# Written first, on row groups: the bias and the push of the expert layer, in a six-stage transformer kernel

## The reference

```python
def _L1_ffn_ref(x, router_w, router_b, expert_w, expert_b):
    logits = jnp.einsum('bsd,ed->bse', x, router_w) + router_b
    probs = jax.nn.softmax(logits, axis=-1)
    weights = jnp.max(probs, axis=-1)
    top1 = jnp.argmax(probs, axis=-1)
    y_all = jnp.einsum('bsd,eod->bseo', x, expert_w) + expert_b
    y = jnp.take_along_axis(y_all, top1[:, :, None, None], axis=2)[:, :, 0, :]
    return y * weights[:, :, None]
...
    x = x + 0.5 * _L0_ffn_ref(_layernorm(x, axis=-1), ...)
    x = x + _L0_attn_ref(_layernorm(x, axis=-1), ...)
    x = x + 0.5 * _L0_ffn_ref(_layernorm(x, axis=-1), ...)
    x = x + 0.5 * _L1_ffn_ref(_layernorm(x, axis=-1), ...)
    x = x + _L1_attn_ref(_layernorm(x, axis=-1), ...)
    x = x + 0.5 * _L1_ffn_ref(_layernorm(x, axis=-1), ...)
```

## Time and profile before

| | us |
|---|---|
| median of 3 runs | 1593.41 (1593.11 to 1596.53) |
| profiled execution | 1591.5, of which the span is 1589.6 |
| first expert stage | about 1181 to 1250 of the span |
| second expert stage | about 1518 to the end of the span |
| TensorE busy (matmul) | 1541.5, 97% |
| VectorE busy | 1260.2, 79% |
| ScalarE busy | 936.1, 59% |
| GpSimd busy | 935.5, 59% |
| one batch of the first expert stage | 8.18 |

### The profile page before, as it was taken

One profiled execution on the slowest core, in us unless ns is written; L12 is line 12 of the kernel. 1 busy time (PEld: TensorE's weight loads), 2 busy tenths in 40 slices (PEclk: granted clock), 3 DMA queues, 4 the chain that ended last, 5 costly groups with the idle time before them and its releaser, 6 DMA issues. The chain is left out here.

```text
span 1589.6 us, 43810 instructions
## 1 busy us (share of the span) xinstructions
PE 1541.5 (97%) x15808; PEld 922.1 (58%) x15808; DVE 1260.2 (79%) x2662; ACT 936.1 (59%) x1826; POOL 935.5 (59%) x806
## 2 busy tenths in 40 slices
PE   7999999999999899799999999999999999999999
PEld 4666666666666666566666666666654434444444
DVE  7976776777877788786777777768778899999877
ACT  6755555555656344365555555556553388888842
POOL 2865756757754399775766756657456334444453
PEclk9999999999999999999999999999999899999999
DMA  4300000000001242100000000000001121112011
GB/s 163 106 8 5 7 0 7 7 0 7 8 1 34 53 84 67 42 6 3 8 1 7 7 0 7 7 0 8 5 12 31 44 61 37 39 39 62 9 42 60
DMA packets 74315, 43.34 MB, mean 27 GB/s; under 512 B 53818, under 2 KB 70842, under 8 KB 74052
## 3 DMA queue, kind: packets, MB, share of 16 engines
q1 hardware_dynamic: 74180, 41.56, 10.9%
HBM read 10.47 MB, written 2.10 MB: 8 GB/s over the span
## 5 line engine op out<-in xcount | busy, mean ns | idle before, releaser
L618 POOL TENSOR_TENSOR scratch<-scratch 128x512 f16<-128x512 f32 x379 | 441.6, 1166 | 375.4 <-ACT scratch L826 375.2
L1395 DVE SCALAR_TENSOR_TENSOR scratch<-psum,scratch 128x512 f32<-128x512 f32 x512 | 352.4, 689 | 235.8 <-PE psum L1979 213.4
L821 ACT ACTIVATE scratch<-psum 128x512 f32<-128x512 f32 x512 | 305.2, 597 | 394.9 <-PE psum L1979 394.0
L2021 PE MATMUL psum<-ffn_down_hi,scratch 128*128 128x128 f16 x2048 | 369.3, 219 | 0.3
L2023 PE MATMUL psum<-ffn_down_hi,scratch 128*128 128x128 f16 x2048 | 369.2, 219 | 0.0
L2022 PE MATMUL psum<-ffn_down_lo,scratch 128*128 128x128 f16 x2048 | 369.2, 219 | 0.0
L826 ACT ACTIVATE scratch<-scratch 128x512 f16<-128x512 f32 x512 | 318.6, 622 | 12.0 <-DVE scratch L1395 11.7
L2021 PEld LDWEIGHTS psum<-ffn_down_hi,scratch 128*128 128x128 f16 x2048 | 200.3, 98 | 59.1 <-POOL scratch L618 0.7
L2022 PEld LDWEIGHTS psum<-ffn_down_lo,scratch 128*128 128x128 f16 x2048 | 200.4, 98 | 58.0
L2023 PEld LDWEIGHTS psum<-ffn_down_hi,scratch 128*128 128x128 f16 x2048 | 200.4, 98 | 0.0
L1977 PE MATMUL psum<-x_hi,ffn_gate_hi 128*128 (+1 forms) x512 | 194.5, 380 | 1.5 <-ACT scratch L821 1.5
(11 more groups left out here) (223 smaller groups left out, 2703.8 us busy)
## 6 DMA issues: line engine op xcount, KB each, us to landing
scratch<-scratch SPq DMA_DIRECT2D x96, 128.0 KB, 2.7
raw<-in_ffn_w_dram SPq DMA_DIRECT2D x8, 768.0 KB, 4.2
ffn_up_hi<-scratch SPq DMA_DIRECT2D x32, 128.0 KB, 2.8
x_tok<-in_x_dram SPq DMA_DIRECT2D x8, 256.0 KB, 7.2
out_dram<-x_tok SPq DMA_DIRECT2D x7, 256.0 KB, 2.2
raw<-in_lin_dram SPq DMA_DIRECT2D x1, 1092.0 KB
x_hi<-scratch SPq DMA_TRANSPOSE x46, 2.3
x_lo<-scratch SPq DMA_TRANSPOSE x46, 2.3
```

Of the source, the lines that this page charges most:

```text
L618: pool.tensor_tensor(h_lo[r], h32[r], h_hi[r], ALU.subtract).then_inc(s_plo, 1)
L821: act.activation(gate_act[k % 2], bank(k % 2), ACT.Silu, scale=W_DOWN).then_inc(s_s, 1)
L1395: dve.scalar_tensor_tensor(h32[k % HSLOTS], bank(5 + k % 2), W_DOWN, gate_act[k % 2], ALU.mult, ALU.mult).then_inc(s_h, 1)
L2021: pe.matmul(dst, h_hi[r][:, cols], hi, start=k % FC == 0 and n == 0, stop=False, skip_group_check=True)
```

## The change

TensorE writes the bias and the push first. They stand in four groups of 32 rows (`E_GROUP`), each with the bias rows of one half (`e_bias`, placed by twelve small DMAs), and one push of four matmuls with 512 columns opens the banks of two tiles; the full products are then added to them (`start=not opened`). The mask `e_not` is written 16 times over, 32 columns apart in four groups of which the first 8 columns hold it, so that its transposition fills the rows of the four groups. Three pairs of banks take turns (`expert_banks`), and `picked_before` gives the pick for which a tile has to wait. The first and last tiles of the first stage, and the batch of the second stage that goes on beside the attention's end, keep another order. VectorE's `select` moves from behind pick 1 to behind pick 0, `prep_bn` from pick 0 to pick 1, `statistics` from pick 2 to pick 1. ScalarE's `x_upper` moves ahead of the first `weigh`, its `others` behind `weigh` 2, with 128 rows instead of 8. GpSimd's `x_lower` moves ahead of `add`. TensorE's loop is written out, and the router's bias is one matmul of 32 columns instead of four of 8.

```diff
-E_OUT = 2.0 ** 15
+E_OUT = 2.0 ** 14
+E_PUSH = 2.0 ** 16 - 2.0 ** 12
+E_GROUP = 32
...
-        e_not = carve(SUB * E, F16)
+        e_not = raw[:, 0:S // 2].bitcast(F16)
+        e_bias = raw[:, S // 2:S // 2 + BANK // 2].bitcast(F16)
...
+        def expert_banks(t):
+
+            if t < 2:
+                return t
+            if t < NS - 3:
+                return (2, 1, 0)[(t - 2) % 3]
+            if t < NS + SUB:
+                return t % 2
+            return (t - NS - SUB) % 3
+
+        def picked_before(t):
+
+            return 3 + max([s for s in range(t) if expert_banks(s) == expert_banks(t)], default=-1)
...
+            turn_x(3, 0)
+            sp.wait_ge(s_erows, 3)
+            sp.wait_ge(s_blo, 2)
+            for i in range(4):
+                c = slice(i % 2 * BANK, (i % 2 + 1) * BANK)
+                row = i * E_GROUP
+                sp.dma_start(e_bias[row:row + E, :], bias_w[0:E, c]).then_inc(s_ebias, 16)
+                sp.dma_start(e_bias[row + E:row + E + 1, :], bias_w[32:33, c]).then_inc(s_ebias, 16)
+                sp.dma_start(e_bias[row + E + 1:row + E + 2, :], bias_w[64:65, c]).then_inc(s_ebias, 16)
+            for b in range(1, NB):
...
                 for b in range(NB):
                     if b:
-                        add(b - 1)
                         if b + 2 < last:
                             x_lower(n0 + SUB * (b + 2))
+                        add(b - 1)
                     if b + 3 < last:
                         prep_rstd(n0 + SUB * (b + 3))
                         norm(b + 3)
...
-                def others(b, odd, at=4):
+                def others(b, odd, at=6):
                     act.wait_ge(s_eoutp, b + 1)
                     if not isinstance(b, int) or b > 1:
                         act.wait_ge(s_ey, SUB * b - SUB)
-                    act.activation(e_out[odd][0:E, :], bank(at)[0:E], ACT.Copy, scale=E_OUT).then_inc(s_eout, 1)
+                    act.activation(e_out[odd], bank(at), ACT.Copy, scale=E_OUT).then_inc(s_eout, 1)
...
-                        if k == 1 and prep and not (isinstance(b, int) and b == 0):
+                        late = use and isinstance(b, int) and b == 1
+                        if k == (1 if late else 0) and prep and not (isinstance(b, int) and b == 0):
                             x_upper(n0 + SUB * b + LEAD)
-                        if k == 3 and more:
+                        if k == 2 and more:
                             others(b0 + b + 1, 1 - odd)
...
-                    dve.tensor_tensor(by(e_not, SUB), by(e_rank, SUB), over(e_first, SUB, E), ALU.not_equal).then_inc(s_enot, 1)
+                    rank = e_rank.rearrange("p (q o e) -> p q o e", q=SUB, o=1).to_broadcast([P, SUB, P // E_GROUP, E])
+                    first = e_first.rearrange("p (q o c) -> p q o c", q=SUB, o=1).to_broadcast([P, SUB, P // E_GROUP, E])
+                    dve.tensor_tensor(e_not.rearrange("p (q o c) -> p q o c", q=SUB, c=E_GROUP)[:, :, :, 0:E], rank, first, ALU.not_equal).then_inc(s_enot, 1)
...
                             route(b0 + b + 1)
-                        if k == 0 and b + 3 < last:
+                            select(b0 + b + 1)
+                        if k == 1 and b + 3 < last:
                             if b + 3 >= NB:
                                 dve.wait_ge(s_eadd, t0 + SUB * (b + 4 - NB) + LEAD)
                             if use:
                                 dve.wait_ge(s_mout, b + 4)
                             prep_bn(n0 + SUB * (b + 3), SUB * ((b + 3) % NB))
-                        if k == 1 and more:
-                            select(b0 + b + 1)
+                            statistics(b + 3)
                         if k == 0 and not more and ph["next"] == ("M",):
                             attention(plan[ph["i"] + 1], 1, False)
-                        if k == 2 and b + 3 < last:
-                            statistics(b + 3)
                         if k == 3 and more:
                             invert_sum(b0 + b + 1)
...
                 def logits(b, s, n):
                     pe.wait_ge(s_xturn, turned(n))
                     pe.wait_ge(s_esh, b)
+                    router_bias = bias_w[:, E * C:E * C + E].rearrange("p (o e) -> p o e", o=1).to_broadcast([P, SUB, E])
+                    pe.matmul(by(bank(7, 0, SUB * E), SUB), ones, router_bias, start=True, stop=True)
                     for q in range(SUB):
-                        dst = bank(7, q * E, (q + 1) * E)
-                        pe.matmul(dst, ones, bias_w[:, E * C:E * C + E], start=True, stop=False)
-                        ins = three(dst, parts(s + q), ecols(E * C, E * C + E), False)
+                        dst, (hi, lo), (w_hi, w_lo) = bank(7, q * E, (q + 1) * E), parts(s + q), ecols(E * C, E * C + E)
+                        pe.matmul(dst, hi, w_hi, start=False, stop=False, skip_group_check=True)
+                        pe.matmul(dst, hi, w_lo, start=False, stop=False, skip_group_check=True)
+                        ins = pe.matmul(dst, lo, w_hi, start=False, stop=True, skip_group_check=True)
                     ins.then_inc(s_elg, 1)
 
-                def products(t, s, k, halves=range(2)):
-                    pe.wait_ge(s_epick, t + 1)
+                def products(t, s, halves=range(2), opened=False):
+                    if not opened:
+                        pe.wait_ge(s_epick, picked_before(t))
                     for half_of in halves:
                         a = half_of * BANK
-                        three(bank(2 * (k % 2) + half_of), parts(s), ecols(a, a + BANK), True, False)
-
-                def bias_and_others(b, k, odd):
-                    if k == 0:
+                        dst, (hi, lo), (w_hi, w_lo) = bank(2 * expert_banks(t) + half_of), parts(s), ecols(a, a + BANK)
+                        pe.matmul(dst, hi, w_hi, start=not opened, stop=False, skip_group_check=True)
+                        pe.matmul(dst, hi, w_lo, start=False, stop=False, skip_group_check=True)
+                        ins = pe.matmul(dst, lo, w_hi, start=False, stop=opened, skip_group_check=True)
+                    if opened:
+                        ins.then_inc(s_ey, 1)
+
+                def bias_and_others(b, tiles, odd, opens=False):
+                    if 0 in tiles:
                         pe.wait_ge(s_eout, b + 1)
-                    for half_of in range(2):
-                        a = half_of * BANK
-                        ins = pe.matmul(bank(2 * (k % 2) + half_of), e_out[odd][:, k * P:(k + 1) * P], bias_w[:, a:a + BANK], start=False, stop=True)
-                    ins.then_inc(s_ey, 1)
-
-                def others(b, at=4):
+                        if b == 0:
+                            pe.wait_ge(s_ebias, 12 * 16)
+                    if opens:
+                        pe.wait_ge(s_epick, picked_before(b * SUB + tiles[-1]))
+                    for i, k in enumerate(tiles):
+                        for half_of in range(2):
+                            rows = slice((2 * i + half_of) * E_GROUP, (2 * i + half_of + 1) * E_GROUP)
+                            ins = pe.matmul(bank(2 * expert_banks(b * SUB + k) + half_of), e_out[odd][rows, k * P:(k + 1) * P], e_bias[rows, :],
+                                            start=opens, stop=not opens, skip_group_check=True)
+                        if not opens:
+                            ins.then_inc(s_ey, 1)
+
+                def others(b, at=6):
                     pe.wait_ge(s_enot, b + 1)
                     pe.wait_ge(s_eout, b)
+                    if b == NB + 2:
+                        pe.wait_ge(s_mout, NB)
                     for k in range(SUB):
-                        ins = pe.matmul(bank(at, k * P, (k + 1) * P)[0:E], e_not[:, k * E:(k + 1) * E], ident16, start=True, stop=True)
+                        ins = pe.matmul(bank(at, k * P, (k + 1) * P), e_not[:, k * P:(k + 1) * P], ident16, start=True, stop=True)
                     ins.then_inc(s_eoutp, 1)
...
                 def body(b, odd, first, more):
                     nx, sx = n0 + SUB * b + LEAD, SUB * b + LEAD
                     for k in range(SUB):
+                        opened = not (use and b == 1)
                         if not (first and k < 2):
-                            products(t0 + b * SUB + k, b * SUB + k, k)
...
-                            bias_and_others(b0 + b, k, odd)
-                        if k == (1 if first else 0) and more:
+                            if not opened:
+                                bias_and_others(b0 + b, (k,), odd)
+                        if k == (0 if opened and not first else 1) and more:
                             logits(b0 + b + 1, sx - SUB, nx)
...
-                        if k == 3 and more:
+                        if k == 2 and more:
                             others(b0 + b + 1)
 
                 if use == 0:
                     body(0, 0, True, True)
-                body(1, 1, False, True)
```

(7 more changed lines are left out.)

40 lines of the change are left out of this document (21 added, 19 removed).

## The result

The changed kernel takes **1606.81 us** (median of 4 runs, 1606.63 to 1607.49) against 1593.26 of the kernel before (4 runs, 1592.54 to 1596.53): ratio 1.0077, 95% interval 1.0062 to 1.0093 (the quotient of the two medians is 1.0085), so 13.5 us slower by the medians. The forecast was 1599.0 with a range up to 1606.0: the direction is right, the size less than half, and the time lies just above the range. Of the profiled executions the span grew by 15.3, from 1589.6 to 1604.9 us.

What follows compares the result with a forecast made beforehand. TensorE was taken as what each expert batch waits for; the first stage's +7.6 and the second's -1.85 gave +5.8 us, 1597.3 from the profiled 1591.5, or 1599 from the median 1593.4; range 1589.5 to 1606.

Steps and rivals of the forecast that it cites:

- TensorE's relief and the loop's gap: Expert stages: fewer matmuls and no 0.43 us loop gap cut TensorE's own work from 7.73 to about 6.5 us a batch.
- The wait for the pair: Expert batches: a push opening two tiles waits for the second tile's older pick, pick 2, making the period 7.92 us.
- The first batch: First expert stage, first batch to second: new first push waits for pick 1 with select ahead of it, +0.8 us.
- The port wait: Expert batches: VectorE's select waits for GpSimd's x_lower and add at SBUF ports, +0.97 us, making the period 8.90.
- Rival C: Expert stages: TensorE's clock falls to 1.2 GHz behind its waits, +15 us; chance 0.08.
- The sum: First expert stage, starts of first picks through the last batch: the terms add to +7.6 us, delaying the attention as much.
- the switch: First expert stage, before the last batch: push of tiles 28 and 29 waits for pick 27, 10.04 against 7.73, +2.3 us.
- the last batch: First expert stage: push of tiles 30 and 31 waits for pick 29, picks 28 to 31 take 6.99 against 6.47, +0.5.
- The second stage: Second expert stage: earlier pick at 1540.48 gives -1.1 us and the following batches -0.75, sum -1.85 us.
- A: Expert stages: no port wait, select slips through, -3.5 us, giving 1589.9 us; chance 0.20.
- B: Expert stages: only e_not is blocked or the add starts late, 0.5 to 0.6 a batch, +1 to +3 us; chance 0.15.
- D: TensorE: pushes don't run at once but take 0.75 to 1.06 us each, +14 to +17 us; chance 0.05.

Runs made afterwards that it cites:

- experiment 1: Kernel before with only TensorE's loop over batches 2 to 5 written out: 1590.91 us, ratio 0.9985.
- experiment 4: Changed kernel with GpSimd's add ahead of x_lower again and ScalarE's x_upper back between the first and second weigh: 1595.88 us, ratio 1.0023.
- experiment 7: On top of experiment 4, 14 extra matmuls in the first batch alone, ahead of the push of tiles 2 and 3: 1596.04 us, ratio 1.0017.
- experiment 8: Changed kernel with a push for one tile at a time, each waiting for its own banks' last pick: 1598.57 us, ratio 1.0039.
- experiment 2: Kernel before with TensorE's loop written out and the new order of VectorE, ScalarE and GpSimd, no push ahead, short mask: 1603.10 us, ratio 1.0062.
- (5): Changed kernel with GpSimd's x_lower and add in the expert stages on 128 columns instead of 512: 1595.96 us, ratio 1.0012.
- experiment 6: Changed kernel with 12 or 24 extra unused matmuls on TensorE ahead of the push of tiles 0 and 1 in most batches: 1609.11 us, ratio 1.0105.
- experiment 10: Changed kernel with a push for one tile at a time and statistics behind pick 2 as before: 1586.47 us, ratio 0.9946.
- experiment 3: Changed kernel with the old order of VectorE, GpSimd and x_upper, long mask and three bank pairs kept: 1596.73 us, ratio 1.0019.

## Why the forecast was right in its direction and short in its size

- **TensorE's relief and the loop's gap**: right. The next product follows a push by 0.33 against 0.32, and router matmuls and gap are as forecast (experiment 1). Right behind a product the push also starts 0.09 late, 0.42 in all; behind a wait that does not count. The Trainium skill, "TensorE: Matmul & The Clock Gate", Part 3, has 3.07 times for four such tiles. 4 x 0.216 / 0.33 is 2.6 with the change of mode behind it, and an estimate from the page's figure is 0.28; the measurement is nearer to the row-built 0.32.
- **The wait for the pair**: right where nothing is blocked. The period is then 8.03 (experiment 4) against 7.92 forecast; pick 2 starts 4.84 into the batch (4.83 forecast), and from a pick to the push it is 1.36 where the forecast took 1.28. The first batch without its low clock is 8.89 (experiment 7) against 8.88. In the loop of the changed kernel itself this wait is there but doesn't set the pace (experiment 8).
- **The port wait**: right, and shown from four sides: by the rows' ends, by the order alone (2), by the order undone (4) and by shorter GpSimd work (5). It costs 1.06 a batch against 0.97 forecast, and with all that hangs on it 10 to 11 us of the time. The Trainium skill, "SBUF — State Buffer", section "Who interferes with whom", says that VectorE and GpSimd share a port pair which one of them holds exclusively. Every row of select that is blocked beside `x_lower` or `add` ends 0.04 to 0.16 us behind it, so there the trace agrees. Beside `norm` and `prep_rstd`, which also read SBUF, select's rows kept their 0.19 and 0.29 (the changed kernel at 1538.20 and 1546.39; at most 0.36 in experiment 2), so for those two the rule does not show here, and the measurement decides. That no block was there in the batch of the earlier trace rows was an accident of the old order.
- **The step that failed: the granted clock behind the new waits, put at nothing in the sum.** Rival C, the low clock, had 0.08, argued from the 0.43 us gaps in each batch, which leave the clock at 1.00. The waits to be compared with were the new ones of 2.1 to 3.3 us. Behind those the clock did fall in the first batch, in two in the middle and in the last, though not behind each (2.12 us at 1222.99 here, and 2.50 at 1244.86 in experiment 4, at 1.00). It is not the alternative to the forecast's mechanism but comes with it. Its own price was also mis-sized, in the other direction: where select is blocked anyway, a late batch slips past the block (experiment 6).
- **The sum**: of the first stage 7.6 were forecast and 13.8 came. 2.2 of the missing 6.2 are the first batch, 1.4 and 1.7 the two slow ones in the middle, of which 0.6 and 0.9 came back in the batches behind them, 0.9 the switch, 1.3 the last batch, 0.2 the regular one. Half of the last batch's 1.3 is not the clock: the forecast took 2.60 from pick 28 to pick 29, and the kernel before had 3.22 there (1242.75 to 1245.97), as has experiment 4 with 3.23. The attention's start added 2.1 that no term stood for.
- **The second stage** was forecast at -1.85 and came to -0.25, counted from the attention's first unit. The pick that stood at 1540.48 is 1.6 earlier (1.1 forecast). From there to the first pick of the last batch it is 42.24 us where 40.36 were before and 39.61 forecast. Of these 2.63 too many 1.46 are a batch in which select was called free and is blocked twice (rows of 0.76 and 1.07; 9.38 us instead of 7.92), and 1.61 a batch with the low clock (10.51 instead of 8.90; 0.57 in the window 1580 to 1584); the other three batches give 0.44 back. The last batch is 0.5 shorter.
- **Rivals A, B, D**: A is right only for the batches behind a slow one, where select slips through, and its sum is off by 0.3 (nine times 0.97 and 0.3 taken from +5.8 leave -3.2, not -3.5); B's half blocks are not the rule; D is out, the pushes run at once.

**What stays open.** What decides whether the clock falls behind a wait of some 2 us, and what sets the level that it has over the first unit of the attention, some 30 us in which TensorE waits for VectorE again and again. The kernel before had 1.00 from 1268 on in its profile; every variant had at least one window of 0.8 or less there, whatever its expert stage did. It may be worth up to 3 us, and may be the reason for the groups of run times in experiment 7, but no run here isolates it.

## What to carry to other kernels

Before an instruction with two SBUF operands is moved on VectorE, lay GpSimd's timeline beside the new place: here the short instructions of `statistics`, one pick earlier or later, decided between 6 us of loss and 7 of gain (experiments 8 and 10). The work taken off TensorE showed only once the blocks and the wait for a pair were gone: experiment 10 is 4.4 us faster than the loop written out alone. When versions with different TensorE programs keep the same period, as 9.0 to 9.1 us here, look for a ring of the other engines. Opening two tiles at once ties both to the later tile's consumer; open each by its own wait if the saving in matmuls is small. And when a change makes an engine wait longer, compare the new waits, not the old gaps, with what the clock did behind waits of that length, and give a fall of the clock a chance and a price even where some of those waits passed without one.

## What the runs showed that I had not expected

- Two losses can cancel: a batch 1.5 us late by the low clock was 1.06 shorter next time, because it fell out of step with GpSimd's work (10.58 + 8.03 against 2 x 9.09).
- The small gap of TensorE's `Fori` loop, 0.43 us a batch, is worth 2.8 us in the whole (experiment 1).
- A stage can be shortened by 2.7 us in the trace without the median of ten runs moving (experiment 7); that the clock at the attention's start hides it is likely and not shown.
- Four versions with different work and waits on TensorE (the changed kernel, experiments 2, 6 and 8) run their blocked batches in 9.0 to 9.1 us, because the ring through GpSimd sets the pace.
- A number can come out as expected by another mechanism: the 7.75 to 7.86 of experiment 3 are a wait for the mask, and not for the pair.
